# First rank stage: three of four adjacency groups in three fp32r products each instead of one fp32 product

## The reference

```
R  = adj + I, each row divided by its sum
Xf = x; Xa = x; Z = 0
for n in 0, 1:
    q = Xa @ W1.T @ W2.T;  k = Xa @ W3.T
    probs = softmax(q @ k.T)                 # 4096 x 4096
    A = the largest probs of each row, until they reach 0.9 in sum, renormalized
    Xf = R @ Xf;  Xa = A @ Xa
    Z += Xf @ U1[n].T + Xa @ U2[n].T
out = layernorm(x + layernorm(x + Z) * g + b)
```

## Time and profile before

| | before |
|---|---|
| time, median of 3 runs | 1665.55 us (1661.55 to 1665.65) |
| time of the profiled execution | 1664.64 us |
| its span | 1662.8 us, mean granted TensorE clock 0.956 |
| busy: TensorE, VectorE, ScalarE, GpSimd | 1531.0, 1266.9, 779.7, 244.0 us |

### The profile page before, as it was taken

How to read it: one execution, slowest core, us unless ns; L and a number is a source line. 1 busy time by engine, 2 the same in 40 slices (tenths; PEclk the granted TensorE clock), 3 DMA queues, 4 the chain that set the end, 5 groups by cost and what they waited for, 6 DMA issues and landing times. The chain is left out here.

```text
span 1662.8 us, 17981 instructions
## 1 busy us (share of the span) xinstructions
PE 1531.0 (92%) x4753; PEld 887.4 (53%) x4753; DVE 1266.9 (76%) x3735; ACT 779.7 (47%) x1237; POOL 244.0 (15%) x283
## 2 busy tenths in 40 slices
PE   7999999979999999998999999998259879899996
PEld 4556556434555555554566666565135445455553
DVE  6788888723677777776799999999868787787664
ACT  4555555412556565564444444444134434445444
POOL 2010210241000000001001111112310221312222
PEclk9999999989999999998999999999569999999998
DMA  7556566644444555555556766672000000000000
GB/s 266 176 154 155 154 171 188 192 180 140 166 173 187 208 208 188 185 202 205 187 155 200 190 182 186 178 177 79 3 2 1 1 8 7 1 7 7 7 7 13
DMA packets 53452, 211.94 MB, mean 127 GB/s; under 512 B 22464, under 2 KB 31232, under 8 KB 32880
## 3 DMA queue, kind: packets, MB, share of 16 engines
q1 hardware_dynamic: 49872, 210.61, 40.7%
q0 software_dynamic: 3488, 0.31, 0.2%
HBM read 206.64 MB, written 4.50 MB: 127 GB/s over the span
## 5 line engine op out<-in xcount | busy, mean ns | idle before, releaser
L1289 ACT ACTIVATE psL<-psL,umax 128x1024 f32<-128x1024 f32 x256 | 278.5, 1088 | 297.1 <-DVE umax L1812 297.0
L1818 DVE MAX8 cand<-psL 128x8 f32<-128x256 f32 (+1 forms) x640 | 372.4, 584 | 57.4 <-PE psL L916 52.1
L915 PE MATMUL psL<-kA,mq 128*128 128x512 f32 x512 | 299.5, 585 | 2.5 <-ACT psL L1289 1.6
L885 PE MATMUL psO<-adj_in,xn 128*128 128x512 f32 x512 | 242.7, 597 | 3.8 <-DMA adj_in<-in_adjT 2.1
L885 PE MATMUL psO<-adj_in,xf 128*128 128x512 f32 x512 | 241.9, 597 | 4.4 <-POOL adj_in L611 4.4
L1097 PE MATMUL psO<-ebuf,xn 128*128 128x512 f32 x512 | 241.5, 593 | 0.5 <-DVE ebuf L2029 0.5
L2029 DVE SCALAR_TENSOR_TENSOR ebuf<-ebuf 128x1024 f32<-128x1024 f32 x128 | 156.7, 1225 | 109.0 <-PE psO L1097 92.2
L1449 ACT ACTIVATE ebuf<-psL 128x1024 f32<-128x1024 f32 x128 | 130.5, 1022 | 187.8 <-PE psL L1143 153.4
L916 PE MATMUL psL<-kB,mq 66*128 66x512 f32 x512 | 203.8, 398 | 0.0
L1398 ACT ACTIVATE ebuf<-psL 128x1024 f32<-128x1024 f32 x128 | 130.9, 1023 | 129.3 <-PE psL L1064 128.9
L1155 PE MATMUL psO<-xf,xa 128*128 128x512 f32 x340 | 167.6, 617 | 5.7 <-DVE xf L2182 5.6
(11 more groups left out here) (341 smaller groups left out, 1962.3 us busy)
## 6 DMA issues: line engine op xcount, KB each, us to landing
adj_in<-in_adjT SPq DMA_DIRECT2D x128, 1024.0 KB, 5.0
adj_in<-in_adj SPq DMA_DIRECT2D x32, 2048.0 KB, 7.6
xaT<-in_xT SPq DMA_DIRECT2D x4, 512.0 KB, 5.4
xa_dram<-xa SPq DMA_DIRECT2D x8, 256.0 KB, 7.8
out<-t SPq DMA_DIRECT2D x8, 256.0 KB, 2.3
list_dram<-ids,place POOLq DMA_INDIRECT x64, 9.3
rel_prob<-cut_dram SPq DMA_DIRECT2D x32, 2.0 KB
cut_dram<-ncut SPq DMA_DIRECT2D x16, 2.0 KB, 8.8
```

The source lines that it names most:

```text
L885: last = nc.tensor.matmul(psO[:], fs[:, j, :], adj_in[:, r % RING, j % JQ, :], start=(j == 0), stop=(j == JT - 1))
L915: nc.tensor.matmul(o, qA[:, t * P:(t + 1) * P], kA[:, c:c + BI], start=True, stop=False)
L1289: nc.scalar.activation(ps[:], ps[:], ACT.Exp, bias=umax[:, bass.ds(i * UB + k, 1)], scale=1.0, accum_out=usum[:, bass.ds(i * UB + k, 1)]). ...
L1818: last = v.max(cand[:, t % 2, at + c * 8:at + c * 8 + 8], psL[(turn + k) % 3][:, c * WIDE:(c + 1) * WIDE])
```

## The change

In 34 of the 48 groups of the six flows (group number g >= 2 and g % 4 < 3: all but each fourth, and not the first two), each of the four parts is split. ScalarE rounds it to fp32r (`split_hi`, into a ring of nine `part_hi`), GpSimd subtracts the rounded part from the part (`split_lo`, into the place of the part itself), and TensorE makes three fp32r products, x_hi * part_hi, x_lo * part_hi and x_hi * part_lo, where it made one fp32 product. `x_hi` and `x_lo` are made of `xn` in the same manner in four pieces of 128 x 1024 (`piece_hi`, `piece_lo`), in units 3 to 6. A part used in unit U is rounded after the exponentials of unit U - 4 (`LEAD`), not before unit 7. GpSimd's instructions for this stage are ordered anew: its list scatters come one at a time with units 15 to 18 after the end of their block, its self additions six units ahead of use. `rank_store` comes two loads later in SyncE's order. The new tiles lie on the places of tiles that step 0 needs only later (`x_hi` on `ebuf`, `x_lo` on `xa`, `part_lo` on `adj_in`, `part_his` on `xf`, `oT`, `yn`, `t2`); `halves` is new. Two pairs of semaphores (`w_ps`/`w_sb`, `h_flag`/`h_flags` of step 0) are merged into one each, with the values waited for changed to match.

```diff
+        with ExitStack() as rounded:
+            def first(name, shape):
+                return rounded.enter_context(nc.sbuf_tensor(name, shape, FP32R))
+            x_hi = first("x_hi", [P, N])
+            x_lo = first("x_lo", [P, N])
+            part_lo = first("part_lo", [P, RING, JQ, BI])
+            part_his = first("part_his", [P, NB + 3, BI])
...
+        halves = sb("halves", [P, 3, BI], FP32R)
...
+        LEAD = 4
+        PIECES = (1, 2, 3, 0)
+        PIECE_AT = {FLOW_FROM + n: n for n in range(NU)}
+        def is_split(a, j):
+            g = a * PARTS + j // JQ
+            return 2 <= g < FLOWS * PARTS and g % 4 < 3
...
+        SELF_AT = {USED_AT[a, a * JQ] - LEAD - 2: a for a in range(FLOWS)}
+        def splits_at(unit):
+            return [n for n, part in enumerate(SPLITS) if max(USED_AT[part] - LEAD, FLOW_FROM + NU) == unit]
...
-                        if n >= 12 and n % FLOWS == 0:
-                            rank_store((n - 12) // FLOWS)
+                        if n >= 14 and (n - 14) % FLOWS == 0:
+                            rank_store((n - 14) // FLOWS)
...
+                def piece_lo(n):
+                    pool.wait_ge(g["split_hi"], n + 1)
+                    pool.sem_inc(met, 1)
+                    c = slice(PIECES[n] * UNIT, (PIECES[n] + 1) * UNIT)
+                    nc.gpsimd.tensor_tensor(x_lo[:, c], xn[:].rearrange("p t d -> p (t d)")[:, c], x_hi[:, c].bitcast(FP32),
+                                            ALU.subtract).then_inc(g["split_lo"], 1)
+                def split_lo(n):
+                    a, j = SPLITS[n]
+                    part = adj_in[:, j // JQ % RING, j % JQ, :]
+                    pool.wait_ge(g["split_hi"], NU + n + 1)
+                    pool.sem_inc(met, 1)
+                    nc.gpsimd.tensor_tensor(part_lo[:, j // JQ % RING, j % JQ, :], part, part_hi(n).bitcast(FP32),
+                                            ALU.subtract).then_inc(g["split_lo"], 1)
...
-                    for i in range(NB):
-                        for a in SELF_BEFORE.get(i, ()):
-                            add_self(a)
-                        list_rows(i)
+                    add_self(0)
+                    for unit in range(NB * UB):
+                        if unit in PIECE_AT:
+                            piece_lo(PIECE_AT[unit])
+                        if unit in SELF_AT and SELF_AT[unit] > 0:
+                            add_self(SELF_AT[unit])
+                        since = unit - UB + 1
+                        if since >= UB and since % UB < TB:
+                            list_part(since // UB - 1, since % UB)
+                        for m in splits_at(unit):
+                            split_lo(m)
+                    for t in range(1, TB):
+                        list_part(NB - 2, t)
+                    list_rows(NB - 1)
...
+                    if s == 0 and is_split(i, j):
+                        n = SPLIT_NO[i, j]
+                        c = slice(j * P, (j + 1) * P)
+                        pe.wait_ge(g["split_lo"], NU + n + 1)
+                        nc.tensor.matmul(psO[:], x_hi[:, c], part_hi(n), start=(j == 0), stop=False)
+                        nc.tensor.matmul(psO[:], x_lo[:, c], part_hi(n), start=False, stop=False)
+                        last = nc.tensor.matmul(psO[:], x_hi[:, c], part_lo[:, r % RING, j % JQ, :],
+                                                start=False, stop=(j == JT - 1))
+                    else:
+                        last = nc.tensor.matmul(psO[:], fs[:, j, :], adj_in[:, r % RING, j % JQ, :],
+                                                start=(j == 0), stop=(j == JT - 1))
...
+                def piece_hi(n):
+                    act.wait_ge(loaded, 16 * LOADS)
+                    c = slice(PIECES[n] * UNIT, (PIECES[n] + 1) * UNIT)
+                    nc.scalar.copy(x_hi[:, c], xn[:].rearrange("p t d -> p (t d)")[:, c]).then_inc(g["split_hi"], 1)
+                def split_hi(n):
+                    a, j = SPLITS[n]
+                    act.wait_ge(g["adj_in"][j // JQ % RING], adj_loads(s, a, j // JQ))
+                    if j // JQ == a:
+                        act.wait_ge(g["self_in"], (a + 1) * TB)
+                    if n >= HI_RING:
+                        b, m = SPLITS[n - HI_RING]
+                        act.wait_ge(g["adj_used"], b * PARTS + m // JQ + 1)
+                    nc.scalar.copy(part_hi(n), adj_in[:, j // JQ % RING, j % JQ, :]).then_inc(g["split_hi"], 1)
...
+                            if s == 0:
+                                if i * UB + k in PIECE_AT:
+                                    piece_hi(PIECE_AT[i * UB + k])
+                                for n in splits_at(i * UB + k):
+                                    split_hi(n)
```

More of the change, by code:

```diff
@@ L112, in gnn_kernel @@
         norm_dram = [nc.dram_tensor(f"norm_dram{s}", [P * T, 1], FP32, kind="Internal").ap() for s in range(STEPS)]
+        with ExitStack() as rounded:
[5 more added lines that the diff above has]
+            part_his = first("part_his", [P, NB + 3, BI])
+        ebuf = sb("ebuf", [P, 4, UNIT])
+        xa = sb("xa", [P, T, D])
+        adj_in = sb("adj_in", [P, RING, JQ, BI])
+        xf = sb("xf", [P, T, D])
+        oT = sb("oT", [D, BI])
+        yn = sb("yn", [P, TB, D])
+        t2 = sb("t2", [P, TB, D])
         xn = sb("xn", [P, T, D])
-        xa = sb("xa", [P, T, D])
-        xf = sb("xf", [P, T, D])
         z = sb("z", [P, T, D])
@@ L261, in gnn_kernel, with part_hi @@
         flowT = z[:].rearrange("p t d -> p (t d)")
+        HI_RING = 9
+        def part_hi(n):
+            return (halves[:, 0, :], halves[:, 1, :], halves[:, 2, :], part_his[:, 8, :], part_his[:, 9, :],
+                    part_his[:, 10, :], part_his[:, 5, :], part_his[:, 6, :], part_his[:, 7, :])[n % HI_RING]
         NAT = N // 4
@@ L292, in gnn_kernel @@
         chain_p = sem("chain_p")
-        w_ps, w_sb = sem("w_ps"), sem("w_sb")
+        w_made = sem("w_made")
         chain_v = sem("chain_v")
@@ L313, in step_sems @@
             names += ["h_gid", "h_x", "h_ref", "h_xt", "h_xts", "h_q", "h_qhi", "h_qlo",
-                      "h_flag", "h_flags", "h_mid", "h_log", "h_cut", "h_norm", "h_out"]
+                      "h_flag", "h_mid", "h_log", "h_cut", "h_norm", "h_out"]
             names += ["m_q_ps", "m_q_hi", "m_q_lo", "m_o_sb"]
@@ L320, in step_sems @@
                 names += ["sum_act", "sum_dve", "xf_scaled"]
+                names += ["split_hi", "split_lo"]
             else:
-                names += ["slot_full", "slot_read", "h_read", "cut_late"]
+                names += ["h_flags", "slot_full", "slot_read", "h_read", "cut_late"]
                 names += ["r_z_ps", "r_zo_sb", "r_zx_sb", "r_z_sb", "m_z_ps", "m_z_add", "var_sb", "rstd_sb", "centred", "normed", "res_sb"]
@@ L377, in gnn_kernel @@
         assert len(ROWS_AT) == FLOWS - 1 and len(set(unit // UB for unit in ROWS_AT)) == FLOWS - 1
+        LEAD = 4
[4 more added lines that the diff above has]
+            return 2 <= g < FLOWS * PARTS and g % 4 < 3
+        USED_AT = {}
+        for unit in range(NB * UB):
+            for j in flow_parts(unit)[1]:
+                USED_AT[flow_parts(unit)[0], j] = unit
+        SPLITS = [(a, j) for a in range(FLOWS) for j in range(JT) if is_split(a, j)]
+        SPLIT_NO = {part: n for n, part in enumerate(SPLITS)}
+        SELF_AT = {USED_AT[a, a * JQ] - LEAD - 2: a for a in range(FLOWS)}
+        def splits_at(unit):
+            return [n for n, part in enumerate(SPLITS) if max(USED_AT[part] - LEAD, FLOW_FROM + NU) == unit]
         def k_bank(u):
@@ L650, in tile_fetch, with list_part @@
                             bounds_check=N - 1, oob_is_err=False).then_inc(g["h_ref"], 16)
-                def list_rows(i):
[L654 to L660, removed]
+                def list_part(i, e):
+                    t = i * TB + e
+                    pool.wait_ge(g["st_place"], i + 1)
+                    nc.gpsimd.indirect_dma_start(
+                        out=list_dram[s], out_offset=bass.IndirectOffsetOnAxis(ap=place[:, t:t + 1], axis=0),
+                        in_=ids[:, t, :], in_offset=None,
+                        bounds_check=N - 1, oob_is_err=False).then_inc(g["listed"], 16)
@@ new lines, in list_rows @@
+                def list_rows(i):
+                    for e in range(TB):
+                        list_part(i, e)
+                def piece_lo(n):
[4 more added lines that the diff above has]
+                                            ALU.subtract).then_inc(g["split_lo"], 1)
@@ L812, in _ @@
             pe.wait_ge(loaded_first, 16 * LOADS_FIRST)
-            nc.tensor.matmul(psQ[:, 0:DA], w1_sb[:], w2T_sb[:], start=True, stop=True).then_inc(w_ps, 1)
-            pe.wait_ge(w_sb, 1)
+            nc.tensor.matmul(psQ[:, 0:DA], w1_sb[:], w2T_sb[:], start=True, stop=True).then_inc(w_made, 1)
+            pe.wait_ge(w_made, 2)
             pe.wait_ge(ready, 2)
@@ L884, in adj_part @@
```

(14 more changed lines are left out.)

6 lines of the change are left out of this document (removed).

## The result

The changed kernel takes 1705.16 us (median of 4, 1704.93 to 1707.78) against 1665.6: ratio 1.0247, 95% interval 1.0228 to 1.0265. It is slower by about 40 us. The direction was forecast (1679); the size was not, and it lies outside the range (1644 to 1701).

What follows compares the result with a forecast made beforehand. TensorE was taken to bound the first rank stage, 2.37 us a unit. Seven blocks slowed by VectorE's waits, TensorE's saving included, add 13 us, the start 0.3, to 1664.6: 1679 us, range 1644 to 1701.

Steps and rivals of the forecast that it cites:

- TensorE's saving: First rank stage: three fp32r products replace one fp32 product, 0.17 us less for each of 136, 23 us in all.
- just fits: ScalarE's 136 roundings at 0.55 us: densest run 16.9 us against 17.4 of TensorE, no reserve.
- GpSimd's own price: GpSimd's 136 subtractions of 128x512 in the first rank stage: 1.28 us each, plus 0.1 to the next.
- (b): Rival: GpSimd's subtractions, at 1.6 us, come last and TensorE waits for part_lo; about 1659 us, chance 0.15.
- The start: First block: TensorE waits 3 us for the first subtractions, 16 products give 2.7 back: +0.3, ends 0 and +4.
- The mechanism: Units 3 to 13: GpSimd's subtractions hold VectorE's small statistics operations, delaying MAX8, exponential and TensorE's bank; +13 us over seven blocks.
- (a): Rival: the gain arrives, W 3 us or less, TensorE sets the pace; about 1649 us, chance 0.30.
- W: VectorE's added wait per block behind GpSimd's subtractions: 7 us, ends 3 and 24; block formula 34.9 + W - 2.2.
- They take strict turns: Read near 1325 us: GpSimd and VectorE operations alternate, even a tiny one waiting for the whole of GpSimd's.
- the hand-run: Eight units stepped through with assumed prices: MAX8 7.2 us later, 0.9 us per unit; 7.5 units a block give W.
- The count of exposed operations: Statistics operations per block reading two SBUF tiles, in units 3 to 13: 22, waiting at most 24 us a block.
- TensorE bears a lag of about 2.4 us: Each block: a psL bank's path takes 4.1 of 6.5 us, so TensorE tolerates about 2.4 us of VectorE's lag.

Runs made afterwards that it cites:

- e2: Changed kernel without GpSimd's 136 part subtractions and without ScalarE's roundings after the ninth part, three products kept: 1642.7 us, ratio 0.9877.
- e1: Changed kernel without GpSimd's 136 subtractions of parts, ScalarE's roundings and TensorE's three products kept: 1645.6 us, ratio 0.990.
- e3: Changed kernel with one more wait, each subtraction of a part waiting until the one before has ended: 1691.6 us, ratio 1.0179.
- e4: Changed kernel with roundings and subtractions kept, but one fp32 product per part instead of three fp32r ones: 1711.3 us, ratio 1.0288.
- e9: Changed kernel with each subtraction made as two of 128x256, each waiting for the one before: 1682.3 us, ratio 1.0106.
- e7: Changed kernel with chained subtractions held beside MAX8, roundings five units ahead, only every second group split (92 parts): 1659.3 us, ratio 0.9976.

## Why the prediction was wrong

**TensorE's saving** (23 us): right; 20.5 by e2. **ScalarE** ("just fits"): right in effect, 0.61 us for a rounding instead of 0.55, with a price not clear of noise (e1, e2). **GpSimd's own price** (1.28 us): right, median 1.284, never held up itself; the rival that GpSimd is last (b) fell, TensorE waited for `part_lo` only 7 us between 35 and 300. **The start** (+0.3): the MAX8 of unit 16 came 2.9 us later than before, within the +4 given as its upper end, but not by the pause that was forecast: before the first split product TensorE's loads stand still for 0.98 us, not 3. In the profiled execution of the changed kernel the granted clock was 0.50 from 25.1 to 31.9 us, where it was 1.00 before; how much of the 2.9 us that is, no run separates.

**The mechanism**, statistics operations held by GpSimd and MAX8 behind them, was right and is shown by e1 (without subtractions no loss), e3, e4 and e9. Two terms of its sum were mis-sized, and the rival (a), that the gain arrives, fell.

The first is W, the wait per block: 7 us forecast, 65.7/7 = 9.4 measured. The step that failed is "They take strict turns", read from the earlier trace rows. There GpSimd's operations waited for one another by semaphore, about 0.08 us apart, and VectorE came in. The subtractions here are queued without a wait on one another. Most of the time VectorE still gets its turn after one of them (55 of 61), but six operations wait through two to seven GpSimd operations, 21.5 us. Single turns would have cost these six 6 x 1.28 = 8 us at most; the other 14 are most of the excess of W over the forecast, (9.4 - 7) x 7 = 17 us. With the wait put in (e3) W is 51.3/7 = 7.3 us, the 7 that the hand-run gave for strict turns. What lets these six wait and not the others stays open: all lie at the end of unit 3 or the start of unit 4 with a list scatter near, and no run takes the scatters away alone. The count of exposed operations, 22 a block, took those with two SBUF inputs, like the held ones in the earlier trace rows and unlike the MAX8 of the earlier trace rows, and was also too small: copies of 128x4 from SBUF to SBUF wait too (`hard`, mean 833 ns against 190 before; `mx`, 843 against 170), and so do the two `tensor_scalar` (`place`, 342 against 170), though they have one input. That 7 came out all the same, with four operations a block left out, is partly luck.

The second term is the tolerance: "TensorE bears a lag of about 2.4 us" in each block, 2.2 after the other terms. Measured blocks are (362.7 - 58.5) x 16/111 = 43.8 us for the changed kernel, 41.9 for e3, 39.9 for e9, and 35.3 for e1; 8.5, 6.5 and 4.6 us more than e1 for W of 9.4, 7.3 and 4.7. So less than 1 us of a block's wait was absorbed, and nearly each microsecond of VectorE's waits is one of the stage. Part of the room had gone with TensorE's faster products: with the old ones (e4) a W of 9.7 makes the block 6.8 us longer than before (44.5 against 37.7), 2.9 absorbed, where the same formula with 2.37 us a unit would let 4.3 be. The bank room of 2.4 us itself no run measures.

By the formula the measured W makes a block 34.9 + 9.4 - 2.2 = 42.1 and seven blocks (42.1 - 37.9) x 7 = 29 us, for the 13 (12.6 before rounding) of the sum: 17 from W. The measured 43.8 makes it 41: another 12 from the tolerance. What TensorE loses at the clock of 0.50 is in these 41. The mean granted clock of 0.94 over 265 us makes about 32 us at 0.50 (it was 1.00 in the rest), in which TensorE, its loads 0.43 us apart instead of 0.23, does what takes it 17 us at 1.00: by this estimate it loses 15 us at most. e1 had none of it (1.00), and how much of it lay on the critical path, no run separates.

## What to carry to other kernels

Before work is moved to GpSimd, look at what VectorE does in those microseconds: here operations of a few elements with two SBUF inputs, and also fp32 copies and `tensor_scalar` of 128x4 from SBUF to SBUF, waited for the rest of a GpSimd operation of 1.28 us, and now and then for several in a row. Put the GpSimd work beside VectorE instructions that are not held (here MAX8 and reductions, see below), keep each piece short (737 instead of 1287 ns took the ratio from 1.0179 to 1.0106, e9), make one wait for the other (from 1.0247 to 1.0179, e3), and give it no more than fits there (92 parts instead of 136 took it from 1.0126 to 0.9976, e7). Slack in an average (VectorE 81% busy) is no slack where the engine runs nearly back to back for a third of each block (before the change it idled 0.07 to 0.23 us a unit in units 5 to 9).

## What the runs showed that I had not expected

- A few small operations of VectorE, all next to a list scatter, are held through up to seven GpSimd operations in a row (5.64 us for one of 128x4), while most get their turn between two queued ones; one wait between the subtractions brought the kernel from 1704 to 1692 us.
- A VectorE copy of 128x4 fp32 with one SBUF input took 833 ns on average, 190 before; a copy of 128x1 (0.15 us), MAX8 over a unit (mean 1227 ns, 1230 before), MATCH_REPLACE8 (175 and 176) and the reductions of 128x96 (242 to 253 in both) ran as ever.
- Of GpSimd and VectorE only VectorE pays in this stage: all 136 subtractions lie between 1.26 and 1.34 us.
- After a stall of TensorE in this stage (4.9 us) its granted clock was 0.50 for 6.8 us, and its loads came 0.43 us apart instead of 0.23.
